# Keys and values in one 128-row product; context weights loaded tile by tile; more PSUM banks in the context phase

## What is computed

```python
q = LN(x) @ Wq + bq ; k = LN(x) @ Wk + bk ; v = LN(x) @ Wv + bv      # 16 query heads, 4 key/value heads of 16
x = x + softmax(q k^T / 4) v @ Wo + bo
x = x + cross_attention(LN(x), ctx_1024, mask, Wq, Wk, Wv, Wo)       # 16 heads of 64, 77 keys
x = x + shared_swiglu(x) + sum over the top 2 of 8 experts
```

## Time and profile before

| | |
|---|---|
| median of 3 runs (range) | 1822.08 us (1818.28 to 1823.5) |
| profiled execution: its time, its span | 1819.93 us, 1818.2 us |
| busy share PE, PEld, DVE, ACT, POOL | 95%, 62%, 77%, 61%, 20% |
| phase_qkv | 0 to about 94 us |
| phase_self_out | 776 to 858 us |
| phase_context | 858 to 920 us |

### The profile page before, as it was taken

The page is one execution under the profiler, slowest core; times in us unless marked ns, Lnnn a source line. Parts: engine busy times, 40 slices in busy tenths (PEclk is TensorE's granted clock), DMA queues, the critical chain, the costliest instruction groups (busy, mean ns, idle before and its releaser), DMA issues. The chain is left out here.

```text
span 1818.2 us, 36799 instructions
## 1 busy us (share of the span) xinstructions
PE 1722.7 (95%) x12076; PEld 1126.1 (62%) x12077; DVE 1398.4 (77%) x2680; ACT 1106.4 (61%) x2298; POOL 367.3 (20%) x435
## 2 busy tenths in 40 slices
PE   6999999999999999969879999997899999999998
PEld 3443333333333333346468999985798888888887
DVE  6589999999999999424568899984758666666663
ACT  2317888888888888912457888884226555555552
POOL 3000000000000000050023222221130455555540
PEclk9959999999999999979999999998999999999999
DMA  5701122111111120053210212114515233333335
GB/s 172 211 10 29 29 38 42 33 29 30 28 29 28 29 42 16 3 189 104 111 41 28 90 42 73 33 32 140 176 56 168 48 53 53 53 54 52 52 53 155
DMA packets 96014, 120.71 MB, mean 66 GB/s; under 512 B 19019, under 2 KB 76799, under 8 KB 94783
## 3 DMA queue, kind: packets, MB, share of 16 engines
q1 hardware_dynamic: 77936, 95.15, 18.6%
q0 software_dynamic: 13920, 19.15, 6.7%
q10 hardware_dynamic: 4047, 4.94, 0.8%
HBM read 71.42 MB, written 42.53 MB: 63 GB/s over the span
## 5 line engine op out<-in xcount | busy, mean ns | idle before, releaser
L494 DVE TENSOR_REDUCE half_max<-psA 128x1 f32<-128x512 f32 x1024 | 633.3, 684 | 17.6 <-PE psA L545 16.5
L526 ACT ACTIVATE PT<-psB 128x1024 f32<-128x1024 f32 x512 | 518.7, 1026 | 129.8 <-PE psB L555 129.6
L545 PE MATMUL psA<-KS,QS 48*128 48x512 f32 x1024 | 399.0, 469 | 8.6 <-PEq L102 6.8
L555 PE MATMUL psB<-QS,KS 50*128 50x512 f32 x1024 | 366.6, 455 | 0.2 <-ACT PT L526 0.2
L574 PE MATMUL psO<-PT,VG 128*32 128x256 f32 x4096 | 328.1, 393 | 4.5 <-ACT OU L516 0.4
L545 PEld LDWEIGHTS psA<-KS,QS 48*128 48x128 f32 x1024 | 163.9, 192 | 227.6 <-DVE half_max L494 163.3
L574 PEld LDWEIGHTS psO<-PT,VG 128*32 128x32 f32 x4096 | 82.0, 108 | 192.3 <-issue 115.1
L1705 PE MATMUL m_psY<-swd_high,m_hT 128*128 128x256 f32 x832 | 176.4, 295 | 12.7 <-DVE m_hT L1840 9.3
L1310 ACT ACTIVATE x_probs<-x_scores,x_neg_max 128x77 f32<-128x77 f32 x512 | 176.6, 360 | 2.7 <-DVE x_neg_max L1216 2.6
L555 PEld LDWEIGHTS psB<-QS,KS 50*128 50x128 f32 x1024 | 145.9, 186 | 13.1 <-ACT PT L526 10.5
L1705 PEld LDWEIGHTS m_psY<-swd_high,m_hT 128*128 128x128 f32 x832 | 136.9, 191 | 23.5 <-DVE m_hT L1840 12.6
(11 more groups left out here) (208 smaller groups left out, 2760.7 us busy)
## 6 DMA issues: line engine op xcount, KB each, us to landing
QS<-q_parts SPq DMA_DIRECT2D x96, 128.0 KB
q_parts<-part SPq DMA_DIRECT2D x16, 512.0 KB, 3.8
OT<-OU SPq DMA_DIRECT2D x32, 256.0 KB, 2.6
mx_kept<-cx_mx SPq DMA_DIRECT2D x4, 1232.0 KB, 8.2
cx_mx<-mx_kept SPq DMA_DIRECT2D x4, 1232.0 KB, 7.1
KS<-k_parts SPq DMA_DIRECT2D x32, 128.0 KB
xf_rows<-XF SPq DMA_DIRECT2D x32, 128.0 KB, 1.7
acc<-X SPq DMA_DIRECT2D x32, 128.0 KB, 1.8
```

Source lines behind the costliest of these rows:

```text
L494: dve.tensor_reduce(half_max[:, h * (TB // 2) + t % (TB // 2), n:n + 1], psA[:, bank_of(slot, 2 * v + r), :], axis=AX.X, op=ALU.max).then_ ...
L526: act.activation(PT[:, k % 4, 2 * a:2 * a + 2, :].rearrange("p h n -> p (h n)"), psB[:, u % 2, :, :].rearrange("p a n -> p (a n)"), ACT.Ex ...
L545: pe.matmul(psA[:, bank_of(slot, m), :], QS[top:top + KQ, slot, h // 2, t * P:(t + 1) * P], KS[top:top + KQ, slot, n * HALF:(n + 1) * HALF ...
L555: mm = pe.matmul(psB[:, u % 2, r, :], KS[top:top + KM, slot, c * P:(c + 1) * P], QS[top:top + KM, slot, a, half * HALF:(half + 1) * HALF], ...
```

## The change

In `phase_qkv` the key and value weights lie side by side in `wkv`, and one product of 128 output rows makes both; it is now the first of the three. ACT adds the value bias while it copies rows 64 to 127 into `vT`, four PE transposes per quad bring them back into `psV`, and one DVE copy per quad writes `VA`. ACT fills `VA`; POOL fills both halves of `KS` at the start. PE's steps are written out instead of looped. In `phase_self_out` the context loads are cut into 9 and issued one by one behind ACT's copy of every odd tile; ACT's loop is written out. In `phase_context` the score and output units use a ring of three bank pairs, and the transposes back a ring of four banks.

```diff
-        wk = sb("wk_sb", [P, KD, NKV * HD])
-        wv = sb("wv_sb", [P, KD, NKV * HD])
+        wkv = sb("wkv_sb", [P, KD, 2 * NKV * HD])
+        vT = sb("vT", [P, HALF])
-        MS = [(0, P), (1, P), (2, NKV * HD)]
+        KROWS, VROWS = slice(0, NKV * HD), slice(NKV * HD, 2 * NKV * HD)
+        MS = [(2, NKV * HD), (0, P), (1, P)]
...
 gpsimd:
-            pool.memset(VA[:, :, :, :], 0.0).then_inc(consts, 1)
-            pool.wait_ge(consts, 4)
-            pool.memset(VA[:, :, :, HD:HD + 1], 1.0).then_inc(consts, 1)
+            for n, top in enumerate((0, ROWS)):
+                pool.wait_ge(consts, 3 + n)
+                pool.memset(T["KS"].bitcast(F32)[top + 2 * HD:top + ROWS, :, :], 1.0).then_inc(consts, 1)
...
-                    if isinstance(i, int) and i in (1, 2):
-                        top = (i - 1) * ROWS
-                        pool.memset(T["KS"].bitcast(F32)[top + 2 * HD:top + ROWS, :, :], 1.0).then_inc(consts, 1)
-                        pool.wait_ge(consts, 5 + i)
...
 vector:
-                    for g in range(NKV):
-                        dve.tensor_tensor(VA[...], psV[...], bv[...], ALU.add).then_inc(va_done, 1)
+                    dve.tensor_copy(VA[:, :, :, :].rearrange("p (g b) t v -> p b g t v", b=B)[:, i // (S // HALF), :, bass.ds(i % (S // HALF) * QUAD, QUAD), 0:HD],
+                                    psV[:, e, 0:QUAD * NKV * HD].rearrange("p (t g d) -> p g t d", t=QUAD, g=NKV)).then_inc(va_done, 1)
...
 scalar:
+            act.wait_ge(consts, 3)
+            act.activation(VA[:, :, :, :].rearrange("p g t v -> p (g t v)"), ident[:, 0:1].to_broadcast([P, NG * TB * VW]),
+                           ACT.Copy, scale=0.0).then_inc(va_set, 1)
+            act.wait_ge(va_set, 1)
+            act.activation(VA[:, :, :, HD:HD + 1].rearrange("p g t v -> p (g t) v"),
+                           ident[:, 0:1].rearrange("p (a v) -> p a v", a=1).to_broadcast([P, NG * TB, 1]),
+                           ACT.Copy, bias=1.0, scale=0.0).then_inc(va_set, 1)
...
+                        if n == 0:
+                            if not peeled(i, 1):
+                                act.wait_ge(v_done, at(i, 1, 0))
+                            act.activation(vT[VROWS, :], psQ[VROWS, m, :], ACT.Identity, bias=bv[VROWS, :]).then_inc(vt_in, 1)
...
 tensor:
-                project(*MS[2])
+                project(2)
...
+                    pe.wait_ge(vt_in, at(i, 1, 1))
                     for q in range(QUAD):
-                        for k in range(KD):
-                            mm = pe.matmul(psV[:, e, q * NKV * HD:(q + 1) * NKV * HD], xnT[:, e, k, q * P:(q + 1) * P], wv[:, k, :],
-                                           start=(k == 0), stop=(k == KD - 1))
+                        mm = pe.transpose(psV[:, e, q * NKV * HD:(q + 1) * NKV * HD], vT[VROWS, q * P:(q + 1) * P], ident[VROWS, VROWS])
                     mm.then_inc(v_done, 1)
-            staggered(pe, NQ, range(3), step)
+            for n in range(NQ + 2):
+                step(lambda lag, n=n: (n - lag, (n - lag) % 2) if 0 <= n - lag < NQ else None)
...
 phase_self_out, scalar:
-            load_context(act, T)
-            copy(0, 0)
-            copy(1, 1)
-            with act.Fori(1, NT // 2) as j:
-                copy(j * 2, 0)
-                copy(j * 2 + 1, 1)
+            for i in range(NT):
+                copy(i, i % 2)
+                if i % 2:
+                    load_context(act, T, i // 2)
...
+CONTEXT_LOADS = 1 + 4 * KD
+def load_context(eng, T, n):
+    if n == 0:
+        eng.dma_start(T["cx_rows"][:, :, :], T["ctx"].rearrange("b s d -> s b d")).then_inc(T["cx_in"], 16)
+    elif n < CONTEXT_LOADS:
+        name, w = (("cx_wk", "Wkx"), ("cx_wq", "WqxT"), ("cx_wv", "Wvx"), ("cx_wo", "Wox"))[(n - 1) // KD]
+        part = (n - 1) % KD
+        rows = T[w].rearrange("(k p) n -> p k n", p=P)
+        size = rows.shape[1] // KD
+        eng.dma_start(T[name][:, part * size:(part + 1) * size, :], rows[:, part * size:(part + 1) * size, :]).then_inc(T["cx_in"], 16)
...
 phase_context:
-        psM = ctx.enter_context(nc.psum_tensor("psMc", [P, 2, 2, HALF], F32))
-        psR = ctx.enter_context(nc.psum_tensor("psRc", [P, 2, HALF], F32))
+        psM = ctx.enter_context(nc.psum_tensor("psMc", [P, 3, 2, HALF], F32))
+        BACK_RING = 4
...
+        def bank_back(n):
+            return psP[:, n % BACK_RING, :] if n % BACK_RING < 2 else psM[:, (n % BACK_RING - 2) // 2, n % 2, :]
...
-                if u >= 2:
-                    pe.wait_ge(low_in, u - 1)
+                if u >= 3:
+                    pe.wait_ge(low_in, u - 2)
...
-                if u < 2:
-                    pe.wait_ge(low_in, UNITS - 1 + u)
+                if u < 3:
+                    pe.wait_ge(low_in, UNITS - 2 + u)
                 else:
-                    pe.wait_ge(p_in[u % 2], u // 2)
+                    pe.wait_ge(p_in[(u - 3) % 2], (u - 3) // 2 + 1)
...
-                if n >= 2:
-                    pe.wait_ge(r_in[n % 2], n // 2)
+                if n >= BACK_RING:
+                    pe.wait_ge(r_in[n % 2], (n - BACK_RING) // 2 + 1)
```

More of the change, by code:

```diff
@@ L129, in phase_qkv @@
         w_loaded = sem("w_loaded")
-        consts = sem("consts")
+        consts, va_set = sem("consts"), sem("va_set")
         stats_done = sem("stats_done")
@@ L162, in _ @@
                 tokens = slice(i % (S // HALF) * HALF, (i % (S // HALF) + 1) * HALF)
-                for m, rows in MS:
-                    sp.wait_ge(low_done, i * NM + m + 1)
+                for n, (m, rows) in enumerate(MS):
+                    sp.wait_ge(low_done, i * NM + n + 1)
                     if m < 2:
@@ L227, in step @@
                         dve.wait_ge(w_loaded, 16 * 5)
-                        dve.wait_ge(consts, 5)
-                    for m, rows in MS:
-                        dve.wait_ge(high_done, at(i, NM, m + 1))
+                        dve.wait_ge(va_set, 2)
+                    for n, (m, rows) in enumerate(MS):
+                        dve.wait_ge(high_done, at(i, NM, n + 1))
                         dve.scalar_tensor_tensor(part[0:rows, e, 1, m, :], psQ[0:rows, m, :], bqk[0:rows, m:m + 1],
@@ L277, in turned, with part1 @@
                                        psT[:, q % 2, 0:KD * P].rearrange("p (k n) -> p k n", k=KD), ACT.Copy).then_inc(xnT_done, 1)
-                def part1(m, rows):
+                def part1(n):
                     if t := quad(2):
                         i, e = t
-                        act.wait_ge(proj_done, at(i, NM, m + 1))
-                        if m == 0 and not peeled(i, 2):
+                        m, rows = MS[n]
+                        act.wait_ge(proj_done, at(i, NM, n + 1))
+                        if n == 0 and not peeled(i, 2):
                             act.wait_ge(stored[e], (i - e) // 2 * NSTORE)
@@ L312, in turn, with project @@
                         tr.then_inc(tr_done, 1)
[L314 removed]
+                def project(n):
                     if t := quad(2):
                         i, e = t
[L317 removed]
+                        m, rows = MS[n]
+                        if n == 0:
                             pe.wait_ge(xnT_done, at(i, QUAD, QUAD))
                         if not peeled(i, 1):
[L322 removed]
+                            pe.wait_ge(low_done, at(i, NM, n + 1 - NM))
+                            if n == 0:
+                                pe.wait_ge(vt_in, at(i, 1, 0))
                         for k in range(KD):
[L324 to L325 removed]
+                            w = wkv[:, k, :] if m == 2 else wq[:, k, m * P:(m + 1) * P]
+                            mm = pe.matmul(psQ[:, m, :], w, xnT[:, e, k, :], start=(k == 0), stop=(k == KD - 1))
                         mm.then_inc(proj_done, 1)
[L328 removed]
+                project(0)
                 turn(0)
                 turn(1)
[L331 removed]
+                project(1)
                 turn(2)
                 turn(3)
[L334 removed]
+                project(2)
                 if t := quad(2):
@@ L879, in _ @@
                 b, pair = divmod(n, NPK // 2)
-                if n >= 2:
-                    pe.wait_ge(r_in[n % 2], n // 2)
+                if n >= BACK_RING:
+                    pe.wait_ge(r_in[n % 2], (n - BACK_RING) // 2 + 1)
                 for half in range(2):
                     for k in range(KD):
-                        mm = pe.transpose(psR[:, n % 2, half * D + k * P:half * D + (k + 1) * P],
+                        mm = pe.transpose(bank_back(n)[:, half * D + k * P:half * D + (k + 1) * P],
                                           VT[:, b, k, (2 * pair + half) * P:(2 * pair + half + 1) * P], ident[:, :])
@@ L889, in back @@
             b, pair = divmod(n, NPK // 2)
-            return VO[:, b, 2 * pair:2 * pair + 2, :], psR[:, n % 2, :].rearrange("p (c n) -> p c n", n=D)
+            return VO[:, b, 2 * pair:2 * pair + 2, :], bank_back(n).rearrange("p (c n) -> p c n", n=D)
         @block.vector
```

51 lines of the change are left out of this document (19 added, 32 removed).

## The result

The changed kernel takes 1805.05 us (median; 1802.03 to 1806.33), the kernel before, run beside it on the same chip, 1822.79. The ratio is 0.9905, with a 95% interval of 0.9883 to 0.9927: 17 us faster, 13 to 21. The forecast was 1799, the range 1787 to 1811.

A forecast was written before the change was run, and what follows sets the result against it. Read phase by phase: stalls, TensorE and the ACT/DVE/POOL loop, `OT` loads, then ring places and stores. Gains 7.6 + 5.0 + 10.4 = 23.0 us from 1819.93 give 1796.9; with 2.15 for the median, 1799; range 1787 to 1811.

The forecast's parts named there:

- rival D: Context phase: more banks do not help the copies or the score loop, 6.5 to 9 us less gain, 1807; 8 in 100.
- C: Projections: the loop through DVE and POOL is shorter than read, TensorE sets the quads, 8.4 us more, 1790.5; 7 in 100.
- A: Projections: idling once per quad drops TensorE's clock to 1.2 GHz, +28 us over six quads, 1827; 4 in 100.
- B: Closing phase: each context load holds one `OT`, 4.4 us a load, 39.8 over nine, 1833, slower than before; 3 in 100.
- the value merge: Projections, steady quads: sixteen value passes go, four transposes come, but the loop keeps its 8.35 us, so 0 gained.
- The tail: Projections, last quad: one value product fewer, -1.5 us; a last store of 512 KB instead of 256, +0.5; together -1.0.
- tile 2's 3.2: Closing phase: TensorE's wait before tile 2 goes, -3.2 us.
- the stops: Closing phase: context loads delay `OT`, stalls of 0.75 us at each of eight loads, +6 us.
- last score unit: Context phase, score loop: three ring places cut each head pair from 2.52 to 2.12 us, 2.8 gained, ending at 886.3.
- from it to the first copy: Context phase: copies into `VO` wait for the `mx_kept` stores, 15.8 us after the last score unit, untouched by the change.
- from there to the last copy's end: Context phase: copies into `VO` by two engines with two places each take 7.5 us, ending at 909.6 instead of 919.96.
- The 0 for all that is unchanged: Phases whose instructions stay as they are, about 1580 of the 1818 us, were costed at nothing.

The follow-up runs named there:

- qkv_only: The kernel before with all of the change's `phase_qkv` and nothing else; 1811.95 us, ratio 0.9952.
- fills_only: The kernel before with only the fills moved: POOL fills both halves of `KS` at the start, ACT fills `VA`; 1815.53 us, ratio 0.9974.
- loads_only: The kernel before with only the context loads cut in nine and issued behind every odd tile; 1815.94 us, ratio 0.9963.
- loads_behind_ot: The changed kernel with the context loads issued by SP, each behind an `OT` load, in 256 KB pieces; 1795.58 us, ratio 0.9842.
- after_padded: The changed kernel with 256 already met waits put before TensorE's first instruction, to shift the program text; 1806.57 us, ratio 0.9910.
- both_mended: The changed kernel with context loads issued by SP behind `OT` loads and the `mx_kept` stores issued in two halves; 1795.66 us, ratio 0.9829.
- changed_again: The changed kernel run once more, unchanged; 1799.90 us, ratio 0.9872 to the kernel before.
- context_only: The kernel before with only the change's rings in `phase_context`; 1817.39 us, ratio 0.9976.

## Why the prediction was right, and where not

**Direction, place and range** held: the time is 6 us above the forecast, inside the range and inside the forecast's own. It is nearer to the 1807 of rival D, though, and the range held in spite of a context phase that gave a third of its term. That C and A did not happen is plain from the turns at 8.2 to 8.5 us and the full clock of the quads: 1.3 to 1.6 us idle in each 8.3 did no harm. The Trainium skill (TensorE: Matmul & The Clock Gate, section "HAM oscillation — how this bites in real kernels") describes kernels that lose the clock in every turn of a loop; its gaps there are 3 to 5 us, and the trace, with shorter ones, doesn't contradict it; but with gaps that much longer, the section spoke less for A than the prediction had it. B needed 3.2 us of stall per load; the worst stop was 1.6. D is the one that came halfway true.

**Projections: right in the main.** Forecast -7.6, measured -6.8, while the fills alone gave 7.0 in their own run. The pair flatters a little: four traces of the old projections took 92.05 to 94.96, six of the new ones 86.57 to 88.49, and the means are 5.8 apart. Single terms: the first product at 13.40 (forecast 13.3), turn 0 at 16.98 (16.4) and 25.38 (24.75), the four transposes 0.39 us from their start to the next product's (0.35). That the value merge is worth next to nothing in a steady quad, because the loop through ACT, DVE and POOL keeps its length, is shown by TensorE's idle 1.3 to 1.6 us ahead of each turn and by the mean period, 8.33 us in `qkv_only` and 8.49 in `fills_only`. The tail was sized wrong: less work ahead of the last store gave 1.7 us (forecast 1.5), but the larger store took 2.1 back (forecast 0.5), so that it lost 0.4 where 1.0 was to be gained; the 1.0 that `qkv_only` is ahead at the last turn makes up for it. One surprise: the first epsilon addition took 0.92 us instead of 0.17, ending with POOL's fill (8.74 and 8.71), which made `rstd` later; the first `bn_stats` beside the same fill took its usual 1.41. That is as the Trainium skill (SBUF — State Buffer, section "Who interferes with whom") has it: operations of VectorE in the two-port mode are held whole, those outside it with a single SBUF input not; the trace agrees with both halves.

**Closing phase: the sum right (-5.0 and -5.1), in part by luck.** From the start of the phase to the first `psR` 6.9 us were gained (forecast 6.8), tile 2's 3.2 as well, the stops cost 7 instead of 6, and 2 more were gained in the rest (forecast 1, for the clock's earlier rise). But the stops were to be eight of 0.75 us, and came as five of 1.1 to 1.6, the bound of 1.1 exceeded. `loads_only`, with the same code, had eight small ones and 2.7 us less in the phase. The size of this term was an average over rhythms that I did not foresee: with `loads_only`'s the phase would have gained 7.8, and `loads_behind_ot` shows that 5.9 us of it were to be had.

**Context phase: the failed step.** Forecast -10.4, measured -3.4. Three terms were off, in us:

| | forecast | measured | too hopeful by |
|---|---|---|---|
| last score unit | 2.8 earlier | 0.3 earlier | 2.4 |
| from it to the first copy | 15.8 | 17.6 | 1.8 |
| from there to the last copy's end | 7.5 | 10.3 | 2.8 |

The first was a misreading: "one unit of a score pair is 1.31 - 0.79 = 0.52" took the difference of a row of eight matmuls and one of four, both with their modelled ends, as the price of a unit, and subtracted that end from the value product as well. The start times tell it without a model: 865.64, 866.88, 868.12 are 1.24 apart, so the pair's two units cost 0.62 each and the value product 1.24. TensorE's work per pair is 2.47, not 2.07, and the 2.52 of before was TensorE itself with 0.05 of waiting. The second term was taken as fixed by SP and the DMA engines; it came 1.8 longer, with a packet of program text in the midst of the stores, and that packet's place hangs on the length of the code (`after_padded`). The third forgot what 5 us of idle time do to TensorE: the transposes behind it ran at the low level for 3.5 us, which cost 1.7 of the 2.8 (`both_mended`, whose copies also start with four groups waiting but at the full clock, needs 8.6 us), and TensorE, with 0.437 per group, not the two copying engines, sets the pace. That the copies wait for the stores, the main claim on this phase, was right, and was the handle for the larger gain.

**Rival D** had 1807 and the reasons "the copies are still 0.7 apart" or "the score loop does not gain". The latter is what happened, the former not: once the clock was up, the copies came every 0.44. So D's time was close, for one of its two reasons and for two things that it did not name, the late landing and the clock under the copies.

**The 0 for all that is unchanged** did not hold in the profiled executions: attention +6.1, the rest -4.4, both by the time that the clock was low. For attention `changed_again` shows that it isn't the change. Together that is 1.7 us less gained in the profile pair (-13.6) than the changed phases gave (15.3).

## What to carry to other kernels

Read the price of a matmul from start times within a steady loop, never by subtracting the merged durations of two rows: that error alone invented 2.4 us. When a ring is widened, ask first what the end of the stretch waits for; here it was a store issued too late, and splitting it gave 7 us, where the ring of four gave 5.2 alone and 4.0 together with the third pair. Loads that may come any time did best behind the critical load, on its queue and in small pieces. And what ends a phase may be a store's landing: the joint product cut 2.6 us of work, and a larger last store took 2.1 of it back.

## What the runs showed of the hardware

- The granted clock in attention stayed at 0.50 for 42.5 to 75 us of almost unbroken matmuls (99% busy) and then rose, at a moment that differs between executions of one program: 0.40 us of time per us.
- 5.0 us of idle TensorE before the copies left the granted clock at 0.51 for the following 3.5 us, and 3.3 us in `context_only` left it low for 6.8; idle 1.3 to 1.6 us per 8.3 us left it at 1.00.
- One 16 KB packet of program text inside 5.05 MB of stores goes with a landing of 13.4 instead of 11.6 us (four traces with, five without); with it the last 1.7 us flow at 25 GB/s, a sixteenth of 402. Moved to the end of the stores it went with 12.1.
- 256 additional waits on a semaphore that is met early moved TensorE's first transposes from 10.55 to 15.54.
- The last store of the projections landed 8.1 us after its issue with 512 KB, 6.0 with 256 KB.
